# Negated mean on VectorE, last weights signed earlier, and attention's input turned two tiles ahead, in a two-layer kernel on one Trainium2 core

## What is computed

```python
x = x + tanh(g_xattn[0]) * L0_xattn(ctx, ctx, _LN(x), ssm_kernel, D)   # long convolution of k*v pairs, times q
x = x + tanh(g_ffn[0])   * L0_ffn(_LN(x), w1, w2, w3)                  # ternary weights, 8-bit activations, 1408 hidden
x = x + tanh(g_xattn[1]) * L1_xattn(_LN(x), ctx, mask)                 # softmax attention over ctx
x = x + tanh(g_ffn[1])   * L1_ffn(_LN(x), w1, w2, w3)                  # weights sign(w)*mean|w|, 8-bit groups, 2048 hidden
```

## Time and profile before

| | |
|---|---|
| runs shown | 729.6, 732.27, 733.1 us; median 732.27 |
| the profiled execution | 732.03 us, its span 730.2 us |
| TensorE busy | 693.4 us (95% of the span) |
| VectorE busy | 607.0 us (83%) |
| ScalarE busy | 372.4 us (51%) |
| GpSimd busy | 326.7 us (45%) |
| mean granted TensorE clock | 0.993 |

### The profile page before, as it was taken

The page is one execution under the profiler, slowest core; times in us unless marked ns, Lnnn a source line. Parts: engine busy times, 40 slices in busy tenths (PEclk is TensorE's granted clock), DMA queues, the critical chain, the costliest instruction groups (busy, mean ns, idle before and its releaser), DMA issues.

```text
span 730.2 us, 9410 instructions
## 1 busy us (share of the span) xinstructions
PE 693.4 (95%) x3162; PEld 388.4 (53%) x3162; DVE 607.0 (83%) x1094; ACT 372.4 (51%) x541; POOL 326.7 (45%) x362
## 2 busy tenths in 40 slices
PE   5999999988889999899989999999999999999897
PEld 3777777766534444466664444444444444444343
DVE  3998888898899998756985899988888888898871
ACT  3255976281366668546887644443444334433430
POOL 5679788878787665467870002211011111110000
PEclk9999999999999999999999999999999999999999
DMA  8563363320046878979554433334223343332133
GB/s 281 195 242 127 107 247 129 116 78 10 7 113 163 161 166 171 206 252 389 169 145 116 101 73 88 84 76 83 56 63 75 86 88 88 72 87 65 37 73 101
DMA packets 140288, 90.97 MB, mean 125 GB/s; under 512 B 118992, under 2 KB 118992, under 8 KB 140240
## 3 DMA queue, kind: packets, MB, share of 16 engines
q1 hardware_dynamic: 138512, 86.35, 44.1%
q0 software_dynamic: 1200, 3.93, 1.6%
q10 hardware_dynamic: 528, 0.09, 0.1%
HBM read 53.04 MB, written 8.47 MB: 84 GB/s over the span
## 4 chain that ended last, share of the span: by engine, by line
PE 65%; DVE 18%; POOL 6%; DMA 4%; ACT 4%; issue 3%; SPq 0%; POOLq 0%; ACTq 0%; DVEq 0%
PE psum L763 26%; PE psum L627 18%; PE psum L780 14%; DVE phase_space L1119 3%; DVE a_scalars L1125 3%; POOL phase_space L290 3%; PE psum L724 2%; PE psum L746 2%; DVE ln_bn L276 2%; DVE a_scalars L1106 1%; DMA phase_space<-in_L_weights 1%; DVE a_scalars L1099 1%; DVE x_sb L1137 1%; DMA x_sb<-x_between 1%; PE psum L615 1%
## 5 line engine op out<-in xcount | busy, mean ns | idle before, releaser
L763 PE MATMUL psum<-phase_space 128*128 128x512 f16 x1024 | 225.3, 381 | 3.9 <-DMA phase_space<-phase_space 3.2
L627 PE MATMUL psum<-phase_space 128*128 128x288 f32 x640 | 165.3, 414 | 14.3 <-DVE phase_space L1258 8.8
L763 PEld LDWEIGHTS psum<-phase_space 128*128 128x128 f16 x1024 | 100.2, 98 | 127.4 <-issue 4.7
L627 PEld LDWEIGHTS psum<-phase_space 128*128 128x128 f32 x640 | 121.3, 194 | 47.2 <-issue 8.8
L602 POOL DMA_DIRECT2D out<-x_sb x15 | 9.5, 630 | 293.9 <-DVE x_sb L1251 293.9
L780 PE MATMUL psum<-phase_space 128*128 128x512 f16 x512 | 112.6, 379 | 0.0
L290 POOL TENSOR_SCALAR phase_space<-x_sb,ln_ag,ln_rs 128x512 f32<-128x512 f32 x48 | 101.2, 2108 | 9.1 <-POOL ln_rs L285 7.4
L690 PE MATMUL psum<-phase_space 128*128 128x512 bf16 (+1 forms) x384 | 79.2, 361 | 4.7 <-DVE phase_space L1119 4.3
L780 PEld LDWEIGHTS psum<-phase_space 128*128 128x128 f16 x512 | 50.1, 98 | 60.4
L1024 ACT ACTIVATE phase_space<-psum,b_scalars 128x512 f32<-128x512 f32 x64 | 43.2, 681 | 74.6 <-PE psum L763 74.2
L1030 ACT ACTIVATE phase_space<-phase_space,magic 128x1024 f32<-128x1024 f32 x32 | 36.5, 1148 | 84.8 <-DVE phase_space L1230 84.8
(11 more groups left out here) (110 smaller groups left out, 1013.3 us busy)
## 6 DMA issues: line engine op xcount, KB each, us to landing
phase_space<-in_L_weights SPq DMA_DIRECT2D x24, 512.0 KB, 4.6
phase_space<-in_L_weights SPq DMA_DIRECT2D x12, 704.0 KB, 7.0
phase_space<-kpad SPq DMA_DIRECT2D x14, 512.0 KB, 4.1
phase_space<-in_context_heads SPq DMA_DIRECT2D x16, 384.0 KB, 4.8
x_sb<-in_x_tiles SPq DMA_DIRECT2D x16, 256.0 KB, 4.6
phase_space<-in_context_turned SPq DMA_DIRECT2D x8, 512.0 KB, 6.2
x_between<-x_sb SPq DMA_DIRECT2D x16, 256.0 KB
x_sb<-x_between SPq DMA_DIRECT2D x16, 256.0 KB, 6.1
```

The source lines that it names most:

```text
L627: last = nc.tensor.matmul(at(bank(4 * hh + lo), 0, [[64, B], [1, NP]]), toep[n % 2][:, hh, (lo - li) * P:(lo - li + 1) * P], kv[n % 2][:, ...
L763: last = nc.tensor.matmul(bank(2 * (m % 3) + w), fb_qT[n % 2][:, kk % 2, kk // 2, :], b_wT[w][:, kk // 2, c * 512:(c + 1) * 512], start=(k ...
```

## The change

- **Norm.** In three of the four stages VectorE writes minus the mean (ln_nm) after the statistics, and GpSimd's ln_norm adds it and multiplies, where it subtracted the mean and multiplied.
- **Start.** The 4-wide part of the first pairs moves from GpSimd to VectorE; so the count s_kv runs one higher. ScalarE squares before it issues four of its loads. The store of the padded taps comes a little later in SyncE's queue.
- **Weights.** One summing of the first weights moves a step earlier. Six chunks of the last weight are loaded into free space and signed in the convolution's steps 10, 11, 11, 14, 14 and 15; the others follow earlier than before, eleven in the attention and none in the second feed-forward.
- **First feed-forward.** Tiles run one less ahead (scale of t+2, statistics of t+3), the hidden tile is made integers and turned before the next x, and the last head's addition comes later.
- **Attention.** at_xT has three buffers; turned are tiles i+2 in step i, normed i+3.
- **Second feed-forward.** Tile 15 is scaled at the end of tile 13 and rounded before tile 14's first silu.

```diff
+                nc.vector.tensor_scalar(ln_nm[:, stage, n:n + 1], ln_ag[:, stage, n, 0:1], -1.0, None, ALU.mult
+                                        ).then_inc(s_ln[stage], 1)
...
-            nc.gpsimd.tensor_scalar(dst, x_sb[:, n, :], ln_ag[:, stage, n, 0:1], ln_rs[:, stage, n:n + 1],
-                                    ALU.subtract, ALU.mult).then_inc(s_done, 1)
+            nc.gpsimd.tensor_scalar(dst, x_sb[:, n, :], ln_nm[:, stage, n:n + 1], ln_rs[:, stage, n:n + 1],
+                                    ALU.add, ALU.mult).then_inc(s_done, 1)
...
+        ABS_STEP[1, 2] = 4
...
+        NBF = 6
+        B_ORDER = tuple(range(2 * PERW, 2 * PERW + NBF)) + tuple(range(2 * PERW)) + tuple(range(2 * PERW + NBF, NBC))
+        B_STEP = {10: (0,), 11: (1, 2), 14: (3, 4), 15: (5,)}
...
@@ SyncE @@
+                def load_b(q):
+                    j = B_ORDER[q]
+                    if q < 2:
+                        sp.wait_ge(s_wr, 8)
+                        sp.wait_ge(s_ws, 8)
+                    else:
+                        sp.wait_ge(s_ba, q - 1)
...
                 for n in range(NT):
...
                     if n + 2 < NT:
                         load_toeplitz(n + 2)
+                    for q in {9: (0, 1), 11: (2,), 12: (3, 4), 15: (5,)}.get(n, ()):
+                        load_b(q)
                     if n >= NT - 2:
                         turn_x(n + 2 - NT)
 
                 for t in range(NT + 1):
+                    if t >= 1:
+                        turn_hidden(t - 1)
                     if t < NT - 2:
                         turn_x(t + 2)
-                    if t >= 1:
-                        turn_hidden(t - 1)
...
-                    if t % 2 == 1 and 3 <= t < NT - 1:
-                        load_b((t - 3) // 2)
+                    if t % 2 == 1 and t < NT - 1:
+                        load_b(NBF + (t - 1) // 2)
...
@@ GpSimd @@
                 for t in range(NT + 1):
-                    if t < NT - 2:
-                        a_integers_x(t + 2)
...
                     if t >= 1:
                         a_integers_h(t - 1)
-                    if t < NT - 4:
-                        a_norm(t + 4)
+                    if t < NT - 2:
+                        a_integers_x(t + 2)
+                    if t < NT - 3:
+                        a_norm(t + 3)
+                    if t == 0:
+                        finish_heads(NT - 1, 1)
...
                 for i in range(NT):
-                    if i + 2 < NT:
-                        c_norm(i + 2)
+                    if i + 3 < NT:
+                        c_norm(i + 3)
@@ TensorE @@
-                    if 1 <= i < NT - 1:
-                        c_turn_x(i + 1)
+                    if i < NT - 2:
+                        c_turn_x(i + 2)
@@ ScalarE @@
                     if n >= NT - 3:
                         a_round_x(n + 3 - NT)
+                    for q in B_STEP.get(n, ()):
+                        sign_b(q)
...
-                    if t < NT - 3:
-                        a_round_x(t + 3)
+                    if 1 <= t < NT - 2:
+                        a_round_x(t + 2)
...
-                    if i >= 3:
-                        sign_b(i + 3)
+                    if 4 <= i < 15:
+                        sign_b(i + 9)
...
                 for n in range(NT):
+                    if n == NT - 2:
+                        fb_round_x(NT - 1)
                     for c in range(NCB):
                         if c > 0 or n not in (1, 2):
                             fb_silu(n, c)
-                        if NT + 3 + NCB * n + c < NBC:
-                            sign_b(NT + 3 + NCB * n + c)
...
+                        if c == 0 and n == NT - 2:
+                            fb_high_x(NT - 1)
@@ VectorE @@
+                dve.wait_ge(s_cx[0], 16)
+                first_kv = kv[0].rearrange("p l g c -> p (l g c)")
+                nc.vector.tensor_tensor(at(first_kv, 32, [[NP, LB * G * B], [1, 4]]),
+                                        at(cx_sb[0], 0, [[EX, LB * G * B], [1, 4]]),
+                                        at(cx_sb[0], 4, [[EX, LB * G * B], [1, 4]]), ALU.mult).then_inc(s_kv, 1)
...
                 for t in range(NT):
                     a_product(t, 0)
+                    if 1 <= t < NT - 2:
+                        a_scale_x(t + 2)
+                    a_product(t, 1)
+                    if t < NT - 3:
+                        a_stats(t + 3)
                     if t == 0:
-                        a_product(0, 1)
                         fold_heads(NT - 1, 1)
-                    if t < NT - 3:
-                        a_scale_x(t + 3)
-                    if t >= 1:
-                        a_product(t, 1)
-                    if t < NT - 4:
-                        a_stats(t + 4)
                     a_product(t, 2)
...
+                    if n == NT - 2:
+                        fb_deq_x(NT - 1)
...
                     for g in range(4):
                         low_h(n, g)
+                    if n == NT - 3:
+                        fb_scale_x(NT - 1)
+                        fb_up_scales(NT - 1)
```

More of the change, by code:

```diff
@@ L140, in flamingo_two_layers @@
         b_in = [view(R_M + k * BCH, [BCH]) for k in range(2)]
+        b_early = [view(R_B + AW + k * BCH, [BCH]) for k in range(2)]
         at_neg = view(R_M + 2048, [B, C])
         mask_u8 = view(R_M + 4096, [B * C // 2], BF16).bitcast(U8)
-        at_xT = [view(R_A + k * L, [LB, P]) for k in range(2)]
+        at_xT = [view(off, [LB, P]) for off in (R_A, R_A + L, R_F + 9728)]
         at_v = [view(R_A + 1024 + k * C, [C]) for k in range(4)]
@@ L425, in _ @@
                 for b in range(2, B):
-                    if b + 2 < B:
-                        load_rows(b + 2)
                     load_memory(b)
                     reload(B + b - 2)
-                    if b >= 4:
-                        load_b(b + 4)
+                    if b < 4:
+                        load_rows(b + 4)
+                    if b >= 3:
+                        load_b(b + 11)
                 reload(NT - 2)
-                load_b(12)
+                load_b(19)
                 reload(NT - 1)
-                for j in range(13, 2 * PERW + 1):
-                    load_b(j)
+                load_b(20)
                 def fb_turn_x(n):
@@ L459, in fb_turn_hidden @@
                                                ).then_inc(h_T[k][half], 16)
+                load_b(21)
                 fb_turn_x(0)
-                load_b(2 * PERW + 1)
+                load_b(22)
                 fb_turn_x(1)
-                for j in range(2 * PERW + 2, NBC):
-                    load_b(j)
+                load_b(23)
                 fb_turn_x(2)
@@ L484, in pairs @@
                     kv_k = kv[k].rearrange("p l g c -> p (l g c)")
[L485 to L487 removed]
+                    last = nc.gpsimd.tensor_tensor(at(kv_k, E, [[NP, rows], [E, 3], [1, E]]),
+                                                   at(cx_sb[k], 0, [[EX, rows], [0, 3], [1, E]]),
+                                                   at(cx_sb[k], 1, [[EX, rows], [1, 3], [1, E]]), ALU.mult)
+                    if n == 0:
+                        last.then_inc(s_kv, 1)
+                        return
                     nc.gpsimd.tensor_tensor(at(kv_k, 32, [[NP, rows], [1, 4]]), at(cx_sb[k], 0, [[EX, rows], [1, 4]]),
@@ L723, in scores @@
                     for c in range(LB):
-                        last = nc.tensor.matmul(bank(2 + i % 2)[:, 0:C], at_xT[i % 2][:, c, :], ctxT[:, i % B, c, :],
+                        last = nc.tensor.matmul(bank(2 + i % 2)[:, 0:C], at_xT[i % 3][:, c, :], ctxT[:, i % B, c, :],
                                                 start=(c == 0), stop=(c == LB - 1))
@@ L953, in _ @@
                               ).then_inc(s_dfirst, 16)
+                square(0)
                 act.dma_start(kp_sb, taps_in).then_inc(s_kin, 16)
@@ L959, in _ @@
                               ).then_inc(s_gate, 16)
-                square(0)
                 norm_q(0)
@@ L996, in _ @@
                         copy_result(NT - 2 + t, 6 + t)
[L997 to L998 removed]
+                    if t % 2 == 1 and t >= 3:
+                        sign_b(NBF + (t - 3) // 2)
                 c_copy_x(0)
```

79 lines of the change are left out of this document (40 added, 39 removed).

## The result

The changed kernel takes 739.1 us (median of 5 runs, 738.7 to 739.9) against 732.0 for the kernel before beside it: ratio 1.011, interval 1.0088 to 1.0133. The forecast was 727.5 with a range of 718 to 739, so the kernel became slower where faster was forecast, and the time lies just outside the range.

A forecast was written before the change was run, and what follows sets the result against it. The prediction took TensorE as the bound, working 693 of 730 us, with many small waits for other engines. Its terms summed to -4.6 against the profiled 732.03, so 727.4, stated as 727.5 us, range 718 to 739.

The forecast's parts named there:

- Rival 1: GpSimd's norm stays at 2.1 us, felt in the convolution's end and the attention: slower, 738 us; chance 0.24.
- rival 3: VectorE's negation blocks on GpSimd, 0.6 us more each, in first feed-forward and attention: 739 us; chance 0.06.
- conv(12): Convolution tile 12: TensorE stands 6.0 us for ScalarE's copy behind late chunk 2, plus 1.7 lower clock: +7.7 us.
- Rival 2: No wait in conv(12), since the chunk lands before ScalarE needs it: 719.7 us; chance 0.10.
- In the stage itself VectorE gets 0.18 per tile more: First feed-forward: the negation adds 2 us in 11 tiles, costed at nothing; up to 2 if the cover is gone.
- I sum this to -1.7: Attention: cheaper norm and hidden copy against late tiles 2 and 4 and two negations per tile: -1.7 us.
- I take 1.5 of it: Convolution's end, gap of 1.9 us at 176.21: 1.5 goes, and 1.7 of lower clock; whole term -4.4 us.
- Turn (-3): Turn from convolution to feed-forward: of TensorE's waits of 4.3 us for VectorE, 3 go: -3 us.
- 80 us (-1.4): TensorE's wait of 1.5 us for ScalarE at 80 us goes, one sum moving from step 5 to 4: -1.4 us.
- reload (+1.2): End of first feed-forward: the reload of x is issued about 1 us later, and VectorE waits for it: +1.2 us.
- end (-1.9): Second feed-forward's last tile arrives 1.0 us earlier, wait 2.87 becomes 1.9, lower clock goes with even chances: -1.9 us.
- silus (-0.7): Second feed-forward: no chunk left to sign between the first silus, so its wait of 0.7 goes: -0.7 us.

The follow-up runs named there:

- experiment 4: The changed kernel with the old subtracting norm on GpSimd and VectorE's negation taken out: 749.9 us, ratio 1.0235.
- experiment 1: The changed kernel with the load of chunk 2 of the last weights issued in step 10 instead of 11: 730.9 us, ratio 0.999.
- experiment 10: The changed kernel with VectorE's maximum over the mask taken over 16 of 256 columns: 739.5 us, ratio 1.0102.
- experiment 3: The changed kernel with the negation on GpSimd instead of VectorE: 734.9 us, ratio 1.004.
- experiment 5: The changed kernel with chunk 2 loaded in step 10, negation on GpSimd, attention's turn one tile ahead, last two chunks' loads ahead of second feed-forward's turns: 723.2 us.
- experiment 8: As experiment 5, but with attention's turn kept two tiles ahead: 727.0 us, ratio 0.9936.
- experiment 11: As experiment 8, with attention's statistics taken one tile earlier on VectorE: 720.6 us, ratio 0.9846.
- experiment 9: As experiment 5, with GpSimd adding the first head before the feed-forward norm at the convolution's last tiles: 718.5 us, ratio 0.9814.
- experiment 7: The kernel before with only the change's add-and-mult norm and VectorE's negation: 729.7 us, ratio 0.9976.

## Why the prediction was wrong

**The norm, the negation (0.74, 0.18 us): right.** 0.82 and 0.154 plus its wait, 0.21 in VectorE's period. Rival 1, which kept the norm at 2.1 us, is false; and so is rival 3, the negation never blocks. The Trainium skill (GPSIMD Engine Reference, Performance versus the Vector engine) gives a body of at most two operations one rate, 1.03 cycles per element. The trace does not agree: the norm with subtract and mult takes 2116 ns (experiment 4) and that with add and mult 816, so the row was the right guide. What makes the slow form slow stays open: the two also differ in the column that they read, ln_ag against ln_nm, and no run separates that from the operation. Experiment 4 is rival 1 made true, and its 10.8 us lie near the 10.4 that rival 1 had summed; that is luck, for the attention alone took 13.2 where the sum had 5.2, and the first feed-forward stage gave 3.8 back.

**conv(12): right in cause, gap 4.8 for 6.0, clock 3.3 for 1.7.** The two errors cancel. One error in the gap is a count. Seven matmuls were put at 0.25 us each by a row that has two records per matmul (20 for the ten of a half), so they take 3.56 us (x14 in the row at 139.51), 1.8 more. TensorE was 1.0 us ahead of the kernel before by then, so that it wanted the copy at 143.07, not at 142.4; and the copy ended at 147.86, not at 148.4. The mechanism was followed correctly, from SyncE's queue to the copy. Rival 2 is false; experiment 1 makes it true, with 8.2 us.

**"In the stage itself VectorE gets 0.18 per tile more, 2 us in 11 tiles, about what it is ahead; I cost it at nothing": the first step that failed, +4.0.** I compared the added work with a cover of one moment. Two questions were not asked. What rate does the engine reach against the one that it feeds? 7.07 us lies under TensorE's 7.12 and 7.28 over it: what was catching up now falls behind in every tile. The prediction named its own sign of being wrong, new waits of TensorE for VectorE in this stage, and it came:

```profile
236.18 4.92 PE L715 MATMUL psum<-phase_space 128*128 128x512 bf16 x23 [0.67 <-DVE phase_space L1149]
...
267.17 4.91 PE L715 MATMUL psum<-phase_space 128*128 128x512 bf16 x24 [1.92 <-DVE phase_space L1149]
```

Its bound of 2 us for a lost cover was too low as well. And what else draws on the same lead? Two one-off pieces: the maximum over the mask (1.84 us of TensorE's time by experiment 10), and GpSimd's mask operation, behind which VectorE's L1162 now stood:

```profile
233.36 1.35 DVE L1162 TENSOR_TENSOR a_scalars<-a_scalars,a_down 128x1 f32<-128x1 f32 x1
```

```profile
229.54 0.14 DVE L1132 TENSOR_TENSOR a_scalars<-a_scalars,a_down 128x1 f32<-128x1 f32 x1
```

(changed kernel, then before.) The fast norm lets GpSimd begin its mask operation (1.90 us in both) while VectorE is at that line, where before the long norm delayed it until the line was past. With the negation off VectorE the stage still loses 2.4 us (experiments 3, 5 and 8), and among its periods ahead of the mask's maximum (8.95 us, as before) the one of 8.0 us is this one; before it was 6.6. With the old norm and no negation the stage loses 0.3 (experiment 4). That L1162 is the cause of the rest is read from the traces; no run moved GpSimd's mask operation.

**"I sum this to -1.7": the second step that failed, +3.2, or +4.9 without the 1.7 that the clock gave back by luck.** I had seen that statistics stay where they are and priced it for tiles 2 and 4 alone, as a start-up loss. It is a loop that returns every other tile (experiment 8's rows) and costs 10.2 us of waits. I counted VectorE's busy time ("36 of 40 us") where the chain counted: with earlier statistics the same VectorE work fitted into 72.6 us instead of 79.8, from attention's first turn to the second feed-forward (experiments 11 and 8). My own sentence that TensorE "wants the normed tile i+2 in step i" should have been followed through one whole step in steady state.

**"I take 1.5 of it" at 176.21: failed, +0.3.** The gap stayed (1.88, now 2.14): GpSimd stood 0.82 us for this tile's statistics before and 2.40 now, so that it waited away what the norm saved, ahead of work that was ready (experiment 9). The lower clock behind the gap did go (1.7), but not as I had reasoned: I had it go with the gap, and the gap is still there.

```profile
182.53 5.12 PE L652 MATMUL psum<-phase_space 128*128 128x288 f32 x20 [2.14 <-POOL phase_space L512]
```

Experiment 7 has the same gap of 2.14 us at this tile, and the low clock behind it. So that part of the term is luck. The term gave -2.5 for -4.4.

**Turn (-3), 80 us (-1.4), reload (+1.2), end (-1.9), silus (-0.7):** -2.9, -1.4, +0.9, -1.7, -0.3; right in size. At the end the tile came only 0.6 us earlier instead of 1.0 (gaps of 1.74 and 0.55 for the one of 2.87), and the lower clock, of which I had counted half, went whole (1.3).

**Start (-0.4): +0.4.** The first matmul did come 0.5 us earlier (8.29 against 8.79); the rest is not by the change (last section).

**The chances.** Two of my three rivals asked what an operation costs; the two failures were in the order of work, and no rival covered them. Against conv(12)'s +7.7 stood gains of 13.5 in seven places, most of them read at a single gap, and a gap's length, with what a lower clock behind it costs, is an upper bound on what its removal brings; 0.45 for faster was too much.

## What to carry to other kernels

An engine that feeds the bottleneck hides added work only while its period stays below the bottleneck's; compare the periods before and after, and list the one-off pieces that draw on the same lead. When a step is moved ahead, move the whole chain that it waits for, and follow the loop through one round in steady state. In a list of loads written out by hand, check for each entry what its queue has ahead of it: one entry one step late was worth 8 us here.

## What I had not expected of the hardware

- **A gap of the same length costs very different amounts.** Gaps of 1.88 (before, tile 15), 2.05 (experiment 10) and 4.84 us were followed by stretches at half clock that cost 1.7, 1.7 and 3.3 us; gaps of 2.12 (before, tile 14), 2.14 and 2.06 us (changed kernel) by none. At tile 15 the same 2.14 us were followed by half clock in experiment 7 and by none in the changed kernel. From the gap alone it cannot be told, and in experiment 10 work that came 1.8 us earlier went with such a stretch. The traces show this for one execution each; of the others only the mean clock is known (0.989 to 0.993 in experiment 10, 0.992 to 0.995 in the changed kernel).
- **The start differs by up to 1.6 us between executions of the same code.** The first matmul of tile 1 came at 22.54 in the changed kernel, at 21.55 in experiment 3, at 21.05 in experiment 4 and at 22.66 in experiment 10, whose start is the same. TensorE's first matmul stood at 8.3 to 8.5 in all four. From there one record followed another at 0.48 us, and from some moment on at 0.24, as at the higher clock later: from 14.2 in the changed kernel, 12.2 in experiment 3 and 11.2 in experiment 4. So the difference is when the pace doubled (the profile has no clock record ahead of that moment). A difference under 1.6 us that arises there says nothing of an edit.
- **VectorE stands behind GpSimd also at its smallest operations.** L1162, one element per partition, took 1.35 instead of 0.14 us behind the mask operation, and in the convolution L1114 took 2.60 instead of 0.68 behind the pairs (2.74). The 128x1 tensor_scalar of L286 held 154 ns in 48 of 48. The Trainium skill (SBUF — State Buffer, "SBUF: two separate sides") says that a VectorE operation with two SBUF inputs blocks fully against a GpSimd operation that reads SBUF. The trace agrees: both lines have two such inputs, and L286 has one.

```profile
162.34 0.68 DVE L1114 TENSOR_TENSOR phase_space<-phase_space 128x512 f32<-128x512 f32 x1
...
166.74 2.60 DVE L1114 TENSOR_TENSOR phase_space<-phase_space 128x512 f32<-128x512 f32 x1
```
